# Layer-norm statistics of the first edge layer computed on ScalarE in two summing passes, with VectorE's scales placed behind its carry comparisons

## The reference

```python
def _layernorm(x, axis=-1, eps=1e-05):
    m = jnp.mean(x, axis=axis, keepdims=True)
    v = jnp.var(x, axis=axis, keepdims=True)
    return (x - m) / jnp.sqrt(v + eps)

# layer 0: one of 8 weights per edge, by the edge's type
h = jnp.maximum(_layernorm(x, axis=-1), 0.0)
xt = jnp.einsum('ni,rio->rno', h, weight)          # weight: 8 x 256 x 256
messages = xt[edge_type, dst]                      # one row per edge
x = x + relu(segment_sum(messages, src, num_segments=50000) + bias)

# layer 1: keep the 32 largest of 256 of h @ W_neigh, mean over the edges into a node
h = jnp.maximum(_layernorm(x, axis=-1), 0.0)
x = x + h @ W_self + segment_sum(maxk(h @ W_neigh)[src], dst) / max(deg, 1)
```

## Time and profile before

| | us |
|---|---|
| median of 3 executions | 3439.34 (3437.35 to 3443.18) |
| the profiled execution: device time | 3443.16 |
| the profiled execution: span of its records | 3441.5 |
| PE, DVE, ACT, POOL busy in the span | 2521.5, 3055.8, 2198.8, 2453.9 |
| mean granted TensorE clock | 0.908 of 2.4 GHz |

### The profile page before, as it was taken

One profiled execution on the slowest core, in us unless ns is written; L12 is line 12 of the kernel. 1 busy time (PEld: TensorE's weight loads), 2 busy tenths in 40 slices (PEclk: granted clock), 3 DMA queues, 4 the chain that ended last, 5 costly groups with the idle time before them and its releaser, 6 DMA issues.

```text
span 3441.5 us, 64743 instructions
## 1 busy us (share of the span) xinstructions
PE 2521.5 (73%) x10738; PEld 1661.2 (48%) x10739; DVE 3055.8 (89%) x13389; ACT 2198.8 (64%) x6002; POOL 2453.9 (71%) x1732
## 2 busy tenths in 40 slices
PE   2665766777678888888867777777777775878777
PEld 1223655555566666666633333333333332656565
DVE  8998778888889999999869999999999998767777
ACT  2995233323333333333359999999999996777777
POOL 0002887767787777878768888888888885767776
PEclk7998888888899999999989999999999998888999
DMA  9701456666655555555545454545545453989998
GB/s 364 282 0 34 81 104 149 143 142 151 134 105 105 102 105 101 107 101 106 92 121 192 174 195 171 189 177 183 183 176 190 171 189 132 299 289 295 304 306 264
DMA packets 308089, 576.91 MB, mean 168 GB/s; under 512 B 32095, under 2 KB 188034, under 8 KB 307982
## 3 DMA queue, kind: packets, MB, share of 16 engines
q1 hardware_dynamic: 212366, 419.40, 35.6%
q0 software_dynamic: 95616, 156.31, 23.5%
HBM read 316.70 MB, written 258.88 MB: 167 GB/s over the span
## 4 chain that ended last, share of the span: by engine, by line
DVE 47%; issue 22%; PE 12%; DMA 9%; POOL 5%; DVEq 3%; ACT 1%; POOLq 1%; SPq 0%; ACTq 0%
DVE best L1163 7%; DVE zone_c L1170 6%; DVE w L1170 6%; DMA agg<-msg,sidx 5%; PE banks L1569 4%; DMA w<-hs,gidx 3%; PE banks L1469 3%; DVE zone_c L1198 3%; DVE zone_c L859 2%; DVE zone_c L1048 2%; DVE stats L894 2%; DVE zone_c L1050 2%; DVE zone_c L1052 2%; DVE zone_c L861 2%; PE banks L1411 2%
## 5 line engine op out<-in xcount | busy, mean ns | idle before, releaser
L1541 PE MATMUL banks<-w,hT 128*128 128x512 f32 x1568 | 761.9, 643 | 252.2 <-ACT hT L1324 247.1
L666 POOL DMA_INDIRECT agg<-msg,sidx x400 | 666.2, 1665 | 200.1 <-issue 116.8
L654 POOL DMA_INDIRECT rows_in<-in_x,gidx x400 | 426.2, 1065 | 435.8 <-DVE gidx L910 305.3
L1541 PEld LDWEIGHTS banks<-w,hT 128*128 128x128 f32 x1568 | 311.8, 204 | 644.3 <-issue 507.3
L1411 PE MATMUL banks<-pick,h 128*128 128x128 f32 x1600 | 287.1, 307 | 312.9 <-ACT h L1215 216.1
L1198 DVE SCALAR_TENSOR_TENSOR zone_c<-banks,rdeg,zone_c 128x256 f32 x784 | 379.4, 484 | 149.3 <-PE banks L1569 114.2
L1569 PE MATMUL banks<-w,zone_c 128*128 x1568 | 405.5, 419 | 134.4 <-POOLq L741 89.8
L1469 PE MATMUL banks<-w,hT 128*128 x1600 | 480.3, 428 | 17.9 <-issue 16.5
L1233 ACT COPY msg<-banks 128x256 f32<-128x256 f32 x400 | 148.0, 370 | 509.4 <-PE banks L1480 491.9
L733 POOL DMA_INDIRECT w<-hs,gidx x392 | 371.4, 947 | 138.2 <-issue 97.0
L1411 PEld LDWEIGHTS banks<-pick,h 128*128 128x128 f32 x1600 | 256.5, 215 | 375.9 <-issue 353.7
(11 more groups left out here) (228 smaller groups left out, 5846.9 us busy)
## 6 DMA issues: line engine op xcount, KB each, us to landing
out_rows<-zone_c SPq DMA_DIRECT2D x196, 512.0 KB, 2.7
agg<-bias SPq DMA_DIRECT2D x2, 25344.0 KB, 97.3
zone_c<-agg SPq DMA_DIRECT2D x98, 512.0 KB, 6.1
hs<-zone_c SPq DMA_DIRECT2D x98, 512.0 KB, 3.6
zone_c<-out_rows SPq DMA_DIRECT2D x98, 512.0 KB, 6.3
rows_in<-in_x SPq DMA_DIRECT2D x97, 512.0 KB, 5.3
keyrow<-key_rows SPq DMA_DIRECT2D x100, 320.0 KB, 4.0
zone_c<-bucket_rows SPq DMA_DIRECT2D x28, 448.0 KB
```

Of the source, the lines that this page charges most:

```text
L654: pool.indirect_dma_start(out=rows_in[p][:, j, :], out_offset=None, in_=x[:, :], in_offset=bass.IndirectOffsetOnAxis(ap=gidx[p][:, j:j + 1 ...
L666: pool.indirect_dma_start(out=agg[:, :], out_offset=bass.IndirectOffsetOnAxis(ap=sidx[p][:, j:j + 1], axis=0), in_=msg[p][:, j * D:(j + 1) ...
L1541: last = mm(bank[4 + j][:, :], hT[p][:, c, j * P:(j + 1) * P], w1[:, c, :], start=(c == 0), stop=(c == KC - 1))
```

## The change

DVE no longer computes mean and variance in the edge layer. ACT sums the four tiles of a batch with a Copy pass (its output goes to `h[p]`, which the Relu pass overwrites later), makes minus the mean, sums the squared deviations with a Square pass, and takes the square root. The three pieces stand between the evictions of messages. DVE makes `rstd` and `shift` at the end of what it does for the edge layer in a batch, behind the carry comparisons and the destinations. The buffers `stats` and `mv` go; one semaphore is replaced by two.

```diff
-            def statistics(b, p, source, stats_sem, var_sem):
-                for j in range(B):
-                    last = v.bn_stats(stats[p][:, j, :], source[p][:, j, :])
-                last.then_inc(stats_sem, 1)
-                wait_alone(dve, stats_sem, b + 1)
-                for j in range(B):
-                    last = v.bn_aggr(mv[p][:, j, :], stats[p][:, j, :])
-                last.then_inc(var_sem, 1)
-
-            def scales(b, p, std_sem, recip_sem, done):
...
                 v.tensor_copy(gidx[p][:, :], from0[:, bass.ds(b * B + 2 * B, B)]).then_inc(staged0, 1)
-                statistics(b, p, rows_in, stats0, var0)
-
-                scales(b, p, std0, recip0, rstd0)
+
+            def edge0_scales(b, r, p):
+
+                dve.wait_ge(std0, b + 1)
+                v.reciprocal(rstd[p][:, :], std[p][:, :]).then_inc(recip0, 1)
+                dve.wait_ge(recip0, b + 1)
+                v.tensor_tensor(shift[p][:, :], minus_mean[p][:, :], rstd[p][:, :], ALU.mult).then_inc(rstd0, 1)
...
-                for part, lag in ((edge0_front, 0), (edge0_cross, 1), (edge0_back, 1)):
+                for part, lag in ((edge0_front, 0), (edge0_cross, 1), (edge0_back, 1), (edge0_scales, 0)):
...
+            def edge0_mean(b, r, p):
+
+                act.wait_ge(gathered0[p], 16 * B * (r + 1))
                 for j in range(B):
-                    last = nc.scalar.activation(h[p][:, j, :], source[p][:, j, :], ACT.Relu,
+                    last = nc.scalar.activation(h[p][:, j, :], rows_in[p][:, j, :], ACT.Copy,
+                                                accum_out=total_n[p][:, j:j + 1])
+                last.then_inc(sum0, 1)
+                act.wait_ge(sum0, b + 1)
+                nc.scalar.mul(minus_mean[p][:, :], total_n[p][:, :], -1.0 / D).then_inc(mean0, 1)
+
+            def edge0_deviation(b, p):
+
+                act.wait_ge(mean0, b + 1)
+                for j in range(B):
+                    last = nc.scalar.activation(act_junk[:, j, :], rows_in[p][:, j, :], ACT.Square,
+                                                bias=minus_mean[p][:, j:j + 1],
+                                                accum_out=squares[p][:, j:j + 1])
+                last.then_inc(var0, 1)
+                act.wait_ge(var0, b + 1)
+                nc.scalar.activation(std[p][:, :], squares[p][:, :], ACT.Sqrt, bias=eps[:, 0:1],
+                                     scale=1.0 / D).then_inc(std0, 1)
+
+            def edge0_normal(b, p):
+
+                act.wait_ge(rstd0, b + 1)
+                for j in range(B):
+                    last = nc.scalar.activation(h[p][:, j, :], rows_in[p][:, j, :], ACT.Relu,
                                                 bias=shift[p][:, j:j + 1], scale=rstd[p][:, j:j + 1])
-                last.then_inc(done, 1)
-
-            def edge0_front(b, p):
-                act.wait_ge(var0, b + 1)
-                nc.scalar.activation(std[p][:, :], mv[p][:, :, 1], ACT.Sqrt, bias=eps[:, 0:1]).then_inc(std0, 1)
-                normalise(b, p, rows_in, rstd0, h0)
+                last.then_inc(h0, 1)
...
                 edge0_evict(b, p, 0)
                 if turn:
                     edge0_turned(b + 1, 1 - p, 0)
+                if front:
+                    edge0_mean(b + 2, r + 1, p)
                 edge0_evict(b, p, 1)
+                if front:
+                    edge0_deviation(b + 2, p)
                 edge0_evict(b, p, 2)
                 if front:
-                    edge0_front(b + 2, p)
+                    edge0_normal(b + 2, p)
                 if turn:
                     edge0_turned(b + 1, 1 - p, 1)
                 edge0_evict(b, p, 3)
...
-            edge0_front(0, 0)
-            edge0_turned(0, 0, 0)
-            edge0_front(1, 1)
-            edge0_turned(0, 0, 1)
+            for k in range(2):
+                edge0_mean(k, 0, k)
+                edge0_deviation(k, k)
+                edge0_normal(k, k)
+                edge0_turned(0, 0, k)
```

More of the change, by code:

```diff
@@ L270, in graph_layers @@
         livekey = two("livekey", [P, B])
-        stats = two("stats", [P, B, 6])
-        mv = two("mv", [P, B, 2])
         std = two("std", [P, B])
@@ L393, in graph_layers @@
         degrees0 = sem("degrees0")
-        stats0 = sem("stats0")
+        sum0 = sem("sum0")
+        mean0 = sem("mean0")
         var0 = sem("var0")
@@ L1210, in _ @@
         def _(act):
-            def normalise(b, p, source, rstd_sem, done):
-                act.wait_ge(rstd_sem, b + 1)
+            def edge0_mean(b, r, p):
+                act.wait_ge(gathered0[p], 16 * B * (r + 1))
                 for j in range(B):
-                    last = nc.scalar.activation(h[p][:, j, :], source[p][:, j, :], ACT.Relu,
-                                                bias=shift[p][:, j:j + 1], scale=rstd[p][:, j:j + 1])
-                last.then_inc(done, 1)
-            def edge0_front(b, p):
-                act.wait_ge(var0, b + 1)
-                nc.scalar.activation(std[p][:, :], mv[p][:, :, 1], ACT.Sqrt, bias=eps[:, 0:1]).then_inc(std0, 1)
-                normalise(b, p, rows_in, rstd0, h0)
+                    last = nc.scalar.activation(h[p][:, j, :], rows_in[p][:, j, :], ACT.Copy,
[17 more added lines that the diff above has]
+                    last = nc.scalar.activation(h[p][:, j, :], rows_in[p][:, j, :], ACT.Relu,
+                                                bias=shift[p][:, j:j + 1], scale=rstd[p][:, j:j + 1])
+                last.then_inc(h0, 1)
             def edge0_turned(b, p, q):
```

## The result

| us | before | after |
|---|---|---|
| median, 8 executions each | 3440.47 (3433.97 to 3448.22) | 3451.92 (3443.09 to 3461.98) |
| ratio, 95% interval | | 1.0035 (1.002 to 1.0049) |
| profiled execution: device time, span | 3443.16, 3441.5 | 3443.09, 3441.4 |

A later comparison of the same two kernels gave 3445.0 (12 executions) against 3443.1 (17) and a ratio of 1.0005 (0.9994 to 1.0017). So the change costs something between nothing and half a per cent (the two intervals together); it wins nothing that shows. The profiled execution of after is the shortest of its first eight, and its span equals that of before.

What follows compares the result with a forecast made beforehand. POOL was taken as the sort phase's bound; the rank phase stalled on landings of adds behind SP's loads. Terms -13 - 14 - 2 + 1.5 - 1 = -28.5 us gave 3414.7 for the profiled execution, median 3411, range 3378 to 3460.

Steps and rivals of the forecast that it cites:

- VectorE is full, but POOL is the bound in the sort phase: Sort phase: both engines full, POOL never stops, so relieving DVE wins 8 to 18 us, taken as 13.
- ACT's added passes: ACT, each batch: Copy sums with mean 1.98 us and Square sums 2.11, raising its work from 4.8 to 8.9 us.
- The thin cover: ACT's loop of 11.7 us, or 13.1 at the slower pace, lies at or under POOL's 13.1 a batch.
- the slow TensorE pace: PE's lower granted clock, 0.84 in the rank phase against 0.94, would lengthen ACT's loop to 13.1 us.
- When h is ready: Relu passes on ACT start some 2.7 us after DVE's wait for rows, as before, if the root is there.
- The rule on the shared ports: Removing DVE's one-input statistics shortens no POOL instruction; floor stays at 13.1 us, sort phase gains only 8 us.
- the floor of 13.14: POOL's time per sort batch, in us, from a stretch without stalls; leaves 0.15 us a batch to win.
- the sum: Adds the parts: sort -13, rank -14, 447 to 592 us -2, start +1.5, end -1; total -28.5 us.
- Nothing to speak of: Rival: rank phase as before, sort phase at its lower end, about 3430 to 3438; 22 in 100.
- The slower rival: ACT's loop between eviction 0 and the next becomes the bound, 13.8 us a batch, 3467; 23 in 100.
- The rank stall mostly vanishes: Rival: rank-phase loads move off POOL's adds, winning 36 us in place of 14, 3389; 12 in 100.
- The new wait of the Copy pass: ACT waits for gathered rows ahead of evictions 1, 2 and 3; 2.2 us to spare, costed at nothing.

Runs made afterwards that it cites:

- e1: Changed kernel with SP's two rank loads also waiting for the scales of the batch before, some 3 us later; 3407.6 us, ratio 0.9894.
- e5: Changed kernel with ACT's sums, squares and Relu passes in one piece behind the eviction of message tile 2; 3553.8 us, ratio 1.0324.
- e2: Changed kernel with rank loads spread: bucket rows wait for the previous batch's scales, high rows for its earlier-counts; 3383.6 us, ratio 0.9835.
- e8: Changed kernel run again unaltered, for a second trace; 3445.0 us, ratio 1.0005 against the kernel before.
- e6: Kernel before, statistics still on VectorE, with carry comparisons and destinations put ahead of them; 3468.0 us, ratio 1.0066.
- e3: Kernel before, with only the high rows' load waiting for the earlier-counts of the batch before; 3416.5 us, ratio 0.9919.
- e4: Changed kernel with VectorE's scales put back ahead of the carry comparisons and destinations; 3437.1 us, ratio 0.9988.
- e7: Changed kernel with GpSimd's gather of tile 3 issued ahead of the add of tile 2; 3406.7 us, ratio 0.9898.
- e9: Changed kernel with both the e2 and e7 edits; 3382.0 us, ratio 0.982.

## Why the prediction was wrong

*VectorE is full, but POOL is the bound in the sort phase:* right. 13 us were forecast, 14.4 came (16.9 in the second trace), and POOL's idle time fell from 0.34 to 0.31 an instruction. DVE lost its 2.3 us a batch and got back a wait for the root of 78.8 / 53 = 1.5.

*ACT's added passes:* right. The Copy and Square rows of after have 404 and 499 ns, with 186 and 190 for the sums, as the earlier trace rows had them, and between the evictions they cost the sort phase nothing that shows. The thin cover held: the fear of the slow TensorE pace had it backwards, for the granted clock of the sort phase rose from 0.94 to 0.97 (see below); in the rank phase it went from 0.84 to 0.83. "When h is ready" was off: forecast some 2.7 us behind DVE's wait for the rows, if the root was there by then. The root was not, and the Relu passes start 4.8 us behind it in the rank phase and 4.0 in the sort phase. By e1 and by the sort phase, which still gained, this was not what cost the time.

*The rule on the shared ports:* the Trainium skill (SBUF — State Buffer, "SBUF: two separate sides") had POOL's instructions no shorter for want of the statistics. The trace agrees: adds 1610 ns and gathers 1015 in the sort phase of after, against 1598 and 1032 in that of before, 12.9 us a batch in both with their gaps. What the prediction hung on the rule, a gain of only 8 us, came of taking the floor of 13.14 from a short stretch where the gathers took 1078; the measured 13.02 lies nearer to the floor of the whole phase, 12.95 in its own sum.

*The step that failed* is in the sum, for the rank phase: "the loads are merely issued earlier against the adds, so that the add caught behind them is caught less long", -14 us. It was +13.7 over 22 steps, some +17 over 28 batches; with +17 in that place its sum gives a median of 3442, where 3451.9 and 3445.0 were measured. The loads did leave earlier, by 2.6 us against the rows. But an earlier burst caught another add, that of tile 0, for longer, and the add that waits for this one, add 2, stands ahead of the last gather. The text had the fact in hand, "some other add falls in the shadow", and used it only to bound the gain; it did not ask which add waits for which landing and what is queued behind it. It said that the adds' stalls were SP's, and then costed SP's new time with a share of the stall instead of placing the loads on POOL's timeline.

*The rivals.* "Nothing to speak of" came nearest for the total, for another reason than its own: its rank phase was unchanged, while here a loss of 14 met a gain of 14. The slower rival named ACT's loop; e5 shows that loop at 14.66 us a batch, but the change does not enter it. "The rank stall mostly vanishes" was the right place with the wrong cure: e2 removes most of it by spacing the loads, and stands 61 us below e8 (3445.0 - 3383.6). The new wait of the Copy pass, costed at nothing, cost little if anything by e6: without it the rank phase is as long (15.53 against 15.59 and 15.71).

*The size.* The range of 3378 to 3460 holds the measured 3451.9, near its edge; the direction was wrong. It holds it by the width that other rivals gave it, and not because this loss was among them.

## What to carry to other kernels

Where one engine's queue releases bulk loads and another's waits for landings, moving an instruction moves the loads: place every DMA that it releases on the timeline of whoever waits for landings, and look at what is queued behind that wait. A burst that stalls such a wait is cured by spacing it (e2, 1.65% below the kernel before, and e3, one line, 0.8%) rather than by moving it (e4). And a busy engine beside one that hardly ever stops gives little when it is relieved: 2.3 us a batch off DVE won 0.27.

## What the runs showed that was not expected

- An add of 128 rows that leaves together with 1.1 MB of loads is awaited for 7.5 us in before (add 1) and for 8.8 in after (add 0, its chain), against 3.9 for an add away from them. In e4 the add that is caught is add 2. With the loads taken apart (e2) the adds wait 0.38 us each in all.
- The granted clock of the sort phase, a mean of the levels 1.2 and 2.4 GHz, rose from 0.94 to 0.97 at the same work, though PE idles hardly less. Its one long wait in most batches has changed place: before it was for `h` at the fold (L1411), in after it is for a message at the carry (L1490). The sort phase of after, and PE's waits in that of before and, below the dots, of after:

```profile
991.00:1694.00 703.00, 590.37 (x3132) 441.06 (x3131) 585.74 (x3091) 458.05 (x1513) 567.84 (x434) 0.97 0.59 106
```

```profile
PE banks L1411 <- ACT h L1215: 91.3, 46, 2.9
...
PE banks L1490 <- ACT msg L1238: 101.0, 54, 4.4
```

e8 has 0.96 there and e7 even 1.00. PE's idle time in the phase is 118 us in before, 113 in after and 121 in e7, but the part of it in single pauses of over 2 us is 81, 50 and 8. Over the eleven traces this part runs from 7 us (e9, clock 0.99) to 164 (e5, 0.93). The clock went with the long pauses and not with the idle time; that they are the cause is not shown. The higher clock won no time here: e7's batches take 12.97 us and e8's 12.98.
- A wait's releaser in the rows can be wrong by name: in the rank phase of after 33.8 us of the adds' idle time are put down to messages, which had been there for some 6 us (median of the stalls). The landing two adds before is what they waited for.
